# Three edits around the hand-over from long convolutions to a token-wise layer: keys split ahead, a maximum by TensorE's turns, and a moved output projection

## The reference

```python
q, k, v = u @ Wq.T + bq, u @ Wk.T + bk, u @ Wv.T + bv       # channel-major
k = causal_conv(k, k_kernel) + k_D * k                       # length 512, by FFT in the reference
kv = k * v
y = (causal_conv(kv, ssm_kernel) + kv * D) * q
x = layernorm(u + y @ Wo.T + bo)
h = square(relu(x @ W_fc.T))                                 # 1024 hidden
s = h @ W_proj.T
# 5 steps: mem = 0.9*mem + s - (mem > 1); count of mem > 1, divided by 5
out = layernorm(x + counts / 5)
```

## Time and profile before

| what | value |
|---|---|
| median of three runs | 859.67 us (856.86 to 860.92) |
| the profiled execution | 861.3 us, span 859.3 us |
| TensorE / VectorE / ScalarE / GpSimd busy | 87% / 83% / 62% / 45% of the span |
| mean granted clock of TensorE | 0.962 |

### The profile page before, as it was taken

One profiled execution on the slowest core, in us unless ns is written; L12 is line 12 of the kernel. 1 busy time (PEld: TensorE's weight loads), 2 busy tenths in 40 slices (PEclk: granted clock), 3 DMA queues, 4 the chain that ended last, 5 costly groups with the idle time before them and its releaser, 6 DMA issues.

```text
span 859.3 us, 26944 instructions
## 1 busy us (share of the span) xinstructions
PE 743.8 (87%) x11392; PEld 545.7 (64%) x11392; DVE 713.3 (83%) x1192; ACT 529.9 (62%) x625; POOL 390.3 (45%) x307
## 2 busy tenths in 40 slices
PE   0067977999999999766699999999999999999993
PEld 0067977999999999765455555555555455555541
DVE  6896755788888888886568999999999999999885
ACT  2382746778878887765255655666555665556661
POOL 0341212223222222322377666876668866677642
PEclk9998988999999999986799999999999999999997
DMA  8994857999999997890100111011110111101001
GB/s 336 342 263 103 189 135 173 210 231 224 222 228 227 226 211 160 187 263 20 49 1 1 50 49 49 5 44 49 49 49 11 37 49 49 49 20 31 25 24 50
DMA packets 55369, 100.71 MB, mean 117 GB/s; under 512 B 5664, under 2 KB 41376, under 8 KB 53280
## 3 DMA queue, kind: packets, MB, share of 16 engines
q1 hardware_dynamic: 53952, 97.94, 44.7%
q10 hardware_dynamic: 1376, 2.23, 0.7%
HBM read 89.92 MB, written 27.01 MB: 136 GB/s over the span
## 4 chain that ended last, share of the span: by engine, by line
PE 44%; DVE 24%; POOL 17%; issue 10%; DMA 2%; ACT 1%; SPq 0%; POOLq 0%; DVEq 0%; ACTq 0%
PE ps L697 16%; PE ps L683 15%; POOL arena L630 14%; DVE arena L1184 7%; PE ps L813 5%; PE ps L820 5%; DVE u_maxima L917 2%; DVE arena L1181 2%; PE ps L794 2%; DVE arena L1141 2%; DVE arena L1166 2%; DVE arena L1160 2%; DVE arena L971 1%; DMA arena<-kpad_dram 1%; PE ps L772 1%
## 5 line engine op out<-in xcount | busy, mean ns | idle before, releaser
L683 PE MATMUL ps<-arena 128*128 128x96 f16 x3072 | 143.2, 211 | 62.2 <-DVE arena L971 50.8
L697 PE MATMUL ps<-arena 128*128 128x64 f16 (+3 forms) x6144 | 172.2, 182 | 23.3 <-issue 8.9
L630 POOL TENSOR_TENSOR arena<-arena 128x512 f16<-128x512 f32 x128 | 178.9, 1429 | 14.9 <-ACT arena L514 14.4
L697 PEld LDWEIGHTS ps<-arena 128*128 128x128 f16 x6144 | 169.7, 97 | 24.5 <-issue 14.7
L683 PEld LDWEIGHTS ps<-arena 128*128 128x128 f16 x3072 | 138.4, 101 | 64.6 <-issue 56.4
L820 PE MATMUL ps<-arena 128*128 128x512 f16 x768 | 173.2, 379 | 2.9 <-POOL arena L630 2.9
L813 PE MATMUL ps<-arena 128*128 128x512 f16 x768 | 170.8, 379 | 3.4 <-DVE arena L1166 2.5
L596 POOL TENSOR_TENSOR arena<-arena 128x512 f16<-128x512 f32 x32 | 38.1, 1190 | 240.4 <-ACT arena L471 240.4
L1173 DVE TENSOR_TENSOR arena<-arena 128x512 f32<-128x512 f32 x128 | 137.7, 1129 | 10.8 <-POOL arena L630 9.0
L510 ACT ACTIVATE arena<-ps,read_factor 128x512 f32<-128x512 f32 x128 | 88.0, 687 | 76.6 <-PE ps L813 59.6
L820 PEld LDWEIGHTS ps<-arena 128*128 128x128 f16 x768 | 74.0, 98 | 90.6 <-POOL arena L630 9.7
(11 more groups left out here) (99 smaller groups left out, 724.9 us busy)
## 6 DMA issues: line engine op xcount, KB each, us to landing
arena<-kpad_dram SPq DMA_DIRECT2D x192, 256.0 KB, 5.8
kpad_dram<-ksplit_dram SPq DMA_DIRECT2D x64, 256.0 KB, 6.2
qy<-in_uT SPq DMA_DIRECT2D x8, 1024.0 KB, 17.2
arena<-in_u SPq DMA_DIRECT2D x16, 512.0 KB, 4.0
out<-arena SPq DMA_DIRECT2D x16, 512.0 KB, 3.0
arena<-in_k SPq DMA_DIRECT2D x2, 512.0 KB, 5.1
ksplit_dram<-arena ACTq DMA_DIRECT2D x2, 512.0 KB, 3.7
arena<-in_wfT SPq DMA_DIRECT2D x1, 1024.0 KB, 8.7
```

The lines of the kernel that those rows point to most:

```text
L630: nc.gpsimd.tensor_tensor(h16[:, 1, f], h_square[:, f % 4], h16[:, 0, f], ALU.subtract).then_inc(h_lo, 1)
L683: last = nc.tensor.matmul(o, u16[:, x, t, tok:tok + P], wcur[:, w, t], start=(k == 0), stop=(k == 3 * DT - 1))
L697: last = nc.tensor.matmul(out[:, ch * COL + delta * B:(ch + 1) * COL], taps(c, tp)[:, delta * P:(delta + 1) * P], data[:, xp, ch * COL:ch ...
```

## The change

Five things are different; nothing else in the instruction streams moves.

1. ScalarE and GpSimd split the keys of group g+1 before the product of group g, and the split waits for a new semaphore that counts keys read (`keys_read`) instead of whole projections read.
2. The loads of the two feed-forward weights go one group earlier, those of the output weights, bias and first two tiles of tokens ahead of the last group's window load.
3. The last maximum over the partitions is made by two TensorE turns with a VectorE reduction between them, no longer by GpSimd. VectorE copies half of the first y.
4. The first sum and its moments are made in four quarters, as the projection's two banks come.
5. `project_out(1)` stands between parts 3 and 4 of `up` of body 0. In body 0, VectorE has `first_sum(1)` behind the square of part 3 and the norm's shift behind that of part 6.

```diff
             for s in range(NG):
...
+                if s == NG - 5:
+                    sp.dma_start(wf_st, wfT.rearrange("(t p) n -> p t n", p=P)).then_inc(ld_wf, 16)
                 if s == NG - 4:
-                    sp.dma_start(wf_st, wfT.rearrange("(t p) n -> p t n", p=P)).then_inc(ld_wf, 16)
+                    sp.dma_start(wp_st, wpT.rearrange("(t p) n -> p t n", p=P)).then_inc(ld_wp, 16)
                 if s == NG - 3:
-                    sp.dma_start(wp_st, wpT.rearrange("(t p) n -> p t n", p=P)).then_inc(ld_wp, 16)
-            sp.dma_start(wo, woT.rearrange("(t p) n -> p t n", p=P)).then_inc(ld_wo, 16)
-            sp.dma_start(bo_b[:, 0:D], bo.partition_broadcast(P)).then_inc(ld_wo, 16)
...
+                    sp.dma_start(wo, woT.rearrange("(t p) n -> p t n", p=P)).then_inc(ld_wo, 16)
+                    sp.dma_start(bo_b[:, 0:D], bo.partition_broadcast(P)).then_inc(ld_wo, 16)
+                    load_u(0, 0)
+                    load_u(1, 1)
...
             def k_part(g):
-                act.wait_ge(proj_read, GPC * (g // GPC + 1))
+                act.wait_ge(keys_read, GPC * (g // GPC + 1))
...
             def step(s, g):
+                if g + 1 < NG:
+                    k_part(g + 1)
                 act.wait_ge(kv_ready, g + 1)
                 nc.scalar.activation(kv16[:, s % 2, 0], kv, ACT.Copy).then_inc(kv_hi, 1)
-                if g + 1 < NG:
-                    k_part(g + 1)
...
             def step(s, base, more):
+                if not (isinstance(base, int) and base + s == NG - 1):
+                    k_part(s + 1, base + s + 1)
                 pool.wait_ge(kv_hi, base + s + 1)
                 nc.gpsimd.tensor_tensor(kv16[:, s % 2, 1], kv, kv16[:, s % 2, 0], ALU.subtract).then_inc(kv_lo, 1)
-                if not (isinstance(base, int) and base + s == NG - 1):
-                    k_part(s + 1, base + s + 1)
...
-            pool.wait_ge(part_max2_done, 1)
-            nc.gpsimd.partition_all_reduce(all_max[:, cF:cF + 3], part_max[:, cF:cF + 3], P, bass.bass_isa.ReduceOp.max
-                                           ).then_inc(all_max2_done, 1)
...
+            pe.wait_ge(id_done, 3)
+            pe.wait_ge(part_max2_done, 1)
+            nc.tensor.transpose(ps[0:3, 0, 0:P], part_max[:, cF:cF + 3], ident[:, :]).then_inc(turned2, 1)
+            pe.wait_ge(spread2, 1)
+            nc.tensor.transpose(ps[:, 1, 0:3], spread_max[0:3, :], ident[0:3, 0:3]).then_inc(all_max2_done, 1)
...
             def body(i, r, left):
-                if left and not (isinstance(i, int) and i == 0):
+                first = isinstance(i, int) and i == 0
+                if left and not first:
                     project_out(i + 1)
                 up(i, r, range(0, 4))
-                if not (isinstance(i, int) and i == 0):
+                if first:
+                    project_out(i + 1)
+                else:
                     turn_counts(i - 1, left)
...
             turn_y(1, 1)
-            project_out(1)
             turn_x(0, 0)
...
             times_q(PAIR - 1, NG - 1)
+            dve.wait_ge(y_ready, NG)
+            nc.vector.tensor_copy(y_seq[:, 0, 2:4], y_by_token[:, 2:4, :, 0]).then_inc(y_first_ready, 1)
+            dve.wait_ge(turned2, 1)
+            link(nc.vector.tensor_reduce(scratch[0:3, 8:9], ps[0:3, 0, 0:P], AX.X, ALU.max))
+            nc.vector.tensor_copy(spread_max[0:3, :], scratch[0:3, 8:9].to_broadcast([3, P])).then_inc(spread2, 1)
             dve.wait_ge(all_max2_done, 1)
+            nc.vector.tensor_copy(all_max[:, 3:6], ps[:, 1, 0:3]).then_inc(all_max2_read, 1)
+            dve.wait_ge(all_max2_read, 1)
...
-            first_sum(0, 0)
+            dve.wait_ge(u_bo_ready, 1)
+            for j in range(NI):
+                dve.wait_ge(wo_first, j // 2 + 1)
+                last = nc.vector.tensor_tensor(sum1[:, j], PN[:, j], u_bo[:, 0, j], ALU.add)
+                last.then_inc(sum_first, 1)
+                dve.wait_ge(sum_first, j + 1)
+                last = nc.vector.bn_stats(bn_parts[:, 0, j], sum1[:, j])
...
                 for f in range(FT):
                     square(i, f)
-                    if f == 2 and not last:
+                    if f == 3 and first:
+                        first_sum(i + 1, 1 - r)
+                    if f == (6 if first else 2) and not last:
                         norm_shift(0, i + 1)
```

More of the change, by code:

```diff
@@ L154, in build @@
         wp16 = part(8, F16, "p (a t n) -> p a t n", a=2, t=FT)
+        spread_max = part(0.5, F32)
         at[0] = 20 * KB
@@ L198, in build @@
             sem(n) for n in ("u_maxima_done", "u_max_done", "scales1", "scale_u", "scales2"))
-        part_max2_done, all_max2_done, scales3 = (sem(n) for n in ("part_max2_done", "all_max2_done", "scales3"))
+        part_max2_done, turned2, spread2, all_max2_done, scales3 = (
+            sem(n) for n in ("part_max2_done", "turned2", "spread2", "all_max2_done", "scales3"))
+        all_max2_read = sem("all_max2_read")
         vlink = sem("vlink")
@@ L218, in build @@
         ld_wcur, ld_wnext, wcur_ready = (sem(n) for n in ("ld_wcur", "ld_wnext", "wcur_ready"))
-        proj, proj_read, k_hi, k_lo = (sem(n) for n in ("proj", "proj_read", "k_hi", "k_lo"))
+        proj, proj_read, keys_read, k_hi, k_lo = (sem(n) for n in ("proj", "proj_read", "keys_read", "k_hi", "k_lo"))
         kv_ready, kv_hi, kv_lo, y_ready = (sem(n) for n in ("kv_ready", "kv_hi", "kv_lo", "y_ready"))
         ld_u_seq = [sem(f"ld_u_seq{n}") for n in range(2)]
-        u_bo_ready, y_first_ready, y_seq_ready, y_turned, yT_ready, wo_done = (
-            sem(n) for n in ("u_bo_ready", "y_first_ready", "y_seq_ready", "y_turned", "yT_ready", "wo_done"))
+        u_bo_ready, y_first_ready, y_seq_ready, y_turned, yT_ready, wo_first, wo_done = (
+            sem(n) for n in ("u_bo_ready", "y_first_ready", "y_seq_ready", "y_turned", "yT_ready", "wo_first", "wo_done"))
         sum1_ready, moments1_ready, root1_ready, shift1_ready, x1_ready = (
@@ L230, in build @@
         moments = [sem(f"moments{n}") for n in range(2)]
+        sum_first, moments_first = (sem(n) for n in ("sum_first", "moments_first"))
         var_eps_ready = [sem(f"var_eps_ready{n}") for n in range(2)]
@@ L360, in _, with load_u @@
                 load_windows2(1, half)
+            def load_u(b, r):
+                sp.dma_start(u_bo[:, r], u[bass.ds(b * NI, NI)].rearrange("i p n -> p i n")).then_inc(ld_u_seq[r], 16)
             for s in range(NG):
@@ L540, in _ @@
             act.wait_ge(y_ready, NG)
-            nc.scalar.activation(y_seq[:, 0], y_by_token[:, :, :, 0], ACT.Copy).then_inc(y_first_ready, 1)
+            nc.scalar.activation(y_seq[:, 0, 0:2], y_by_token[:, 0:2, :, 0], ACT.Copy).then_inc(y_first_ready, 1)
             y_turn(0)
@@ L777, in turn_y @@
                 if isinstance(i, int) and i == 0:
-                    pe.wait_ge(y_first_ready, 1)
+                    pe.wait_ge(y_first_ready, 2)
                 else:
@@ L795, in project_out @@
                                                 wo[:, t], start=(t == 0), stop=(t == DT - 1))
-                last.then_inc(wo_done, 1)
+                    if isinstance(i, int) and i == 0 and j % 2:
+                        last.then_inc(wo_first, 1)
+                if not (isinstance(i, int) and i == 0):
+                    last.then_inc(wo_done, 1)
             def turn_x(i, r, y_before=True):
@@ L869, in body @@
                 down_second(1)
-            pe.wait_ge(id_done, 3)
+            pe.wait_ge(all_max2_read, 1)
             turn_y(0, 0)
@@ L1142, in norm_factors @@
                 last.then_inc(moments[half], 1)
-                dve.wait_ge(moments[half], i + 1)
+                dve.wait_ge(moments[half], i + 1 - (1 - half))
                 nc.vector.memset(cell[:, half:half + 1], 0.0)
@@ L1155, in first_sum @@
             def first_sum(i, r):
-                dve.wait_ge(wo_done, i + 1)
+                dve.wait_ge(wo_done, i)
                 dve.wait_ge(u_bo_ready, i + 1)
@@ L1194, in second_sum @@
                 norm_factors(1, i, x2)
-            first_sum(0, 0)
+            dve.wait_ge(u_bo_ready, 1)
[5 more added lines that the diff above has]
+                last = nc.vector.bn_stats(bn_parts[:, 0, j], sum1[:, j])
+                last.then_inc(moments_first, 1)
+                dve.wait_ge(moments_first, j + 1)
+                last = nc.vector.bn_aggr(mean_var[:, 0, j], bn_parts[:, 0, j])
+            last.then_inc(moments1_ready, 1)
+            nc.vector.memset(cell[:, 0:1], 0.0).then_inc(sum1_ready, 1)
             norm_shift(0, 0)
@@ L1203, in body @@
             def body(i, r, first, last):
-                if not last:
+                if not last and not first:
                     first_sum(i + 1, 1 - r)
```

6 lines of the change are left out of this document (1 added, 5 removed).

## The result

The changed kernel takes 866.85 us (median of five runs, 864.58 to 867.15) against 859.67 before. The ratio of the two is 1.0073, with a 95% interval of 1.0055 to 1.0090. The likeliest case of the prediction, +3.3 us, was too small. What came true is the fourth in its first half, the last window load that comes too late; of its second half, copies of VectorE behind a gather, one copy of two did.

What follows compares the result with a forecast made beforehand. TensorE's start of body 1 was taken to bound the kernel. First-layer terms sum to -5.75 us; body 0 then puts body 1 at 451.0 against 447.72, +3.3, so 859.67 becomes 863.0; range 857.5 to 867.0 for 8 in 10.

Steps and rivals of the forecast that it cites:

- The likeliest case: Whole kernel: the early start of the first layer is used up by GpSimd's queue; +3.3 us, 863.0, chance 0.50.
- the fourth: Rival: last window load pushed back 2.5 us, or VectorE's copies wait out a full gather, or both; +5.5 to +6.7, chance 0.26.
- the signs that the prediction set itself: Trace marks, among them first layer near 419.5 at half clock, last window load near 378, low parts 2 to 4 us later.
- What bounds the kernel: Token part: whatever shifts TensorE's start of body 1 (447.72) passes to the end at full price; nothing later absorbs it.
- The first body: Body 0: GpSimd's eight low parts wait for the second tile's root, start at 435.2; body 1 starts at 451.0, +3.3 us.
- the clock term: Head of body 0: TensorE starts at half clock, which lengthens its first four parts by 2.5 us.
- The moved projection as a whole: Second output projection: leaves the path to the first layer, gaining 4.1 us; takes 3.5 us in body 0.
- The gain of 4.1 us: Hand-over: with the second projection moved, x1 is turned as soon as ready, not 4.1 us later (417.62 to 421.75).
- The first norm by quarters and the root: Hand-over: moments 2.1 us after the projection instead of 3.11, gain 1.0; root follows at once, gain 2.6.
- The maximum by turns: Hand-over: y turned 0.25 us earlier, VectorE's copies lose half of one gather, +1.0; net +0.75 us.
- Keys split ahead and the loads: End of first part: last window load between 2.06 us earlier and 2.5 us later, taken as +0.3; vanished waits bring nothing.
- The load term: End of first part: the +0.3 us taken for the arrival of the last window load.

Runs made afterwards that it cites:

- e2: Changed kernel with GpSimd's root of the second tile behind its fourth low part of body 0 instead of ahead of the first; ratio 1.0044 to the kernel before.
- e8: Kernel before with only the second output projection moved behind the fourth part of body 0, VectorE's first sum and shift along; ratio 1.0071 to the kernel before.
- e3: Changed kernel with the second output projection back ahead of the turn of x1, VectorE's first sum and shift back too; ratio 0.9971 to the kernel before.
- e9: Changed kernel with second projection and loads back, first key split behind the next weights' first copy, first gather behind VectorE's last scale; ratio 0.9923 to the kernel before.
- e5: Changed kernel with GpSimd's first gather waiting until the maximum has been read; ratio 1.0083 to the kernel before.
- e1: Changed kernel with the weight, bias and token loads issued where they were before; ratio 1.0031 to the kernel before.
- e11: Kernel before with only the loads moved one group earlier; ratio 1.0021 to the kernel before.
- e12: Kernel before with only the key split ahead and its wait on the keys read; ratio 0.9995 to the kernel before.
- e4: Changed kernel with the key split behind the product's split again, waiting on the projection read; ratio 1.0063 to the kernel before.
- e7: Changed kernel with second projection and loads back, gather behind the maximum, first key split behind the first copy of the next weights; ratio 0.9949 to the kernel before.

## Why the prediction came out too low, by its steps

By the signs that the prediction set itself, its likeliest case did not hold: the last window load was to end near 378 and landed after 380 (381.52), and the first low part was to start 2 to 4 us later and started 6.2 later. The first layer was to start at 419.5 and started at 422.04. The whole excess is ahead of that point.

**What bounds the kernel.** Right: body 1's start moved by 5.84 us and the span by 5.3; nothing later absorbed it, and nothing in the loop changed.

**The first body.** Right in mechanism and size. From the start of the first layer to that of body 1 I had 31.5 us, and it took 31.5 (422.04 to 453.56); that the sum meets it to the tenth is luck, since the low parts started 16.1 us after the first layer where I had 15.7, and the rest was 0.4 shorter. The root ahead of the eight low parts in GpSimd's queue held them; e2 shows that this is one holder of two. The size of the clock term was 2.5 and came out at about 2.7 (8.0 us against 5.3).

**The moved projection as a whole.** The prediction booked its gain in one paragraph and its cost in another, and so never said that this one edit costs 6 us alone. e8 measures it, and e3 shows that without it the change would have been a gain. The gain of 4.1 us that I booked to the move is not the move's in this kernel: I took for it the second projection of the kernel before, at 415.24 and with 6.68 us. In e3, where it stays ahead, it starts at 414.33, takes 3.69 us, and x1 is turned at 417.94, as soon as ScalarE has it (417.89).

**The first norm by quarters and the root.** Right: 2.1 us against 2.1 expected, and the root at once.

**The maximum by turns.** From VectorE's last product to the first projection it took 14.88 us (390.45 to 405.33), before 13.91 (387.69 to 401.60): +0.97 against +0.75. The half of a gather that I took for the copies was nearly a whole one on one copy (1.62 us), while the other, the half of y, took 0.71 us, against 0.59 with no gather beside it (e9). The rule of the Trainium skill ("SBUF — State Buffer", "Who interferes with whom"), by which such a copy and a GpSimd operation exclude each other for a whole instruction, agrees with the trace for this float32 copy of three rows: 1.62 us beside the gather, 0.21 without it in e5. In e5 the same is seen on two scale operations on three integer columns (1.88 and 1.84 us), which took 0.17 each in e9.

**Keys split ahead and the loads.** This is the step that failed: "I take +0.3". It belongs to an edit that the title, with its three edits, doesn't name: the loads. VectorE's last product was 2.76 us later. Within it, 1.15 us was there at 157 us already (the projection at 156.06 before starts at 157.21), ahead of the moved loads, and lies within what executions differ by. The other 1.6 came up after it. The move of the loads alone is measured at 3.6 us in e1 and 1.8 us in e11 by the ratios, and at 2.7 and 1.8 by the distance to the last product, where my bounds were -2.06 and +2.5. With the loads back, e1 has a distance 1.1 us shorter than that of the kernel before, and so 2.7 for the loads less 1.1 gives the 1.6 seen here. Whether the 1.1 come from the key split ahead stays open: in e12, with the split alone, the distance is only 0.3 shorter and the total the same. I had reckoned that the hole of 1 us in the DMA queue and an earlier request would nearly pay for one more megabyte ahead of the last windows. They did not: the cost is about the 2.5 us that the fourth case has for a whole weight load. The argument that the 8.0 us of waits were worth nothing was right (e12): the releaser changed, not the time.

**The sum.** The load term came out 2.5 us larger and the maximum 0.2: +3.3 becomes +6.0, against the 5.84 measured at the start of body 1. By the ratio the whole is 6.3 us. Of these 5.84 the 1.15 us from ahead of 157 us may be chance, so the agreement to 0.2 us is in part luck. The fourth case was also added up wrongly: a whole weight load gives 3.3 - 0.3 + 2.5 = +5.5, with the full gather on top +6.4 and not +6.7, and the full gather alone +4.2, which its bounds leave out.

## What to carry to other kernels

An edit that starts a stage earlier by moving work into it has to be costed up to the start of the next stage, through every queue that the moved work feeds: here GpSimd's root and ScalarE's relu stood ahead of independent work, and 3.3 us won became 6 lost. Waits that disappear from one releaser in the list of waits show nothing until the next releaser is named. Small operations of VectorE on the path can each cost nearly the whole length of the GpSimd copy beside them (1.6 to 1.9 us for 0.2 here), and a wait put on GpSimd has to be placed behind the last of them, not the first.

## What the runs showed that I had not expected

The key split of group 0 starts 1.2 us earlier in the changed kernel, since it waits for keys alone, and so runs beside VectorE's first copy of the next weights. The changed kernel (L596 the split, L1020 the copy, L685 the projection that waits for it):

```profile
71.48 1.26 POOL L596 TENSOR_TENSOR arena<-arena 128x512 f16<-128x512 f32 x1 [7.99 <-ACT arena L462]
71.91 0.95 DVE L1020 COPY arena<-arena 128x384 f16<-128x384 f16 x1
...
72.92 5.79 PE L685 MATMUL ps<-arena 128*128 128x96 f16 x96 [2.97 <-DVE arena L1020]
```

and the kernel before:

```profile
71.87 0.25 DVE L1007 COPY arena<-arena 128x384 f16<-128x384 f16 x1
...
72.18 5.85 PE L683 MATMUL ps<-arena 128*128 128x96 f16 x96 [2.27 <-DVE arena L1007]
...
72.70 1.27 POOL L591 TENSOR_TENSOR arena<-arena 128x512 f16<-128x512 f32 x1 [9.24 <-ACT arena L457]
```

The copy took 0.95 us instead of 0.25, and ended 0.74 us later; the projection started 0.74 us later. The split beside it is the cause: the copy took 0.95 us in e12 too, which has only the split ahead, and 0.25 in e4, e7 and e9, where the first split starts behind it. What it costs in the end is not shown: the projection at 116.02 in the kernel before starts at 116.14 in the changed one, so the 0.74 us were 0.12 by then.

The first projection brought TensorE's clock back to full before the second was due in e3 (3.69 us for it), 2.3 us after the end of the first; in the kernel before it comes 7.0 us after it and takes 6.68. The time at which the same work comes changed its price by 3 us.
